# Attention output and the third normalisation in one stage, with a ring of four sets in the attention

## What is computed

```python
def _L1_attn_ref(x, w_q, w_k, w_v, w_o):
    ...
    scores = jnp.einsum('bhqd,bhkd->bhqk', q, k) / jnp.sqrt(jnp.float32(D_K))
    attn = jax.nn.softmax(scores, axis=-1)
    out = jnp.einsum('bhqk,bhkd->bhqd', attn, v)
    out = out.transpose(0, 2, 1, 3).reshape(B, S, HIDDEN)
    return jnp.einsum('bse,oe->bso', out, w_o)
...
x = _layernorm(x + _L1_attn_ref(x, ...), axis=-1)
x = _layernorm(x + _L1_ffn_ref(x, w1, w1_scale, w3, w3_scale, w2, w2_scale), axis=-1)
```

## Time and profile before

| what | us |
|---|---|
| median of 3 runs | 2102.09 |
| the profiled execution | 2091.79 |
| its span, first to last instruction | 2090.1 |
| attention, first score matmul to last quotient | 1025.8 to 1445.4 |
| attention output, first transpose to last sum | 1445.8 to 1501.6 |
| third normalisation | 1501.9 to 1571.4 |
| MLP, from its first matmul | 1571.7 to the end |

### The profile page before, as it was taken

How to read it: one execution, slowest core, us unless ns; L and a number is a source line. 1 busy time by engine, 2 the same in 40 slices (tenths; PEclk the granted TensorE clock), 3 DMA queues, 4 the chain that set the end, 5 groups by cost and what they waited for, 6 DMA issues and landing times. The chain is left out here.

```text
span 2090.1 us, 24698 instructions
## 1 busy us (share of the span) xinstructions
PE 1727.8 (83%) x7763; PEld 1052.6 (50%) x7763; DVE 1571.3 (75%) x2847; ACT 839.0 (40%) x1404; POOL 783.8 (38%) x467
## 2 busy tenths in 40 slices
PE   5888878675698994399688888888728999999998
PEld 1232323223376883288433333334616787778786
DVE  6999999998537996821288888884596667766668
ACT  5646464443114773122157777775231111111112
POOL 4898989892235996420110000000024213311200
PEclk8999989998799997599789999999858999999999
DMA  4343343320126995355533333330001000000002
GB/s 131 98 119 114 103 126 90 92 69 32 57 111 272 411 411 196 112 198 196 174 92 87 94 94 92 87 87 4 32 0 61 28 4 31 31 1 31 1 1 81
DMA packets 110653, 211.59 MB, mean 101 GB/s; under 512 B 18890, under 2 KB 35658, under 8 KB 109628
## 3 DMA queue, kind: packets, MB, share of 16 engines
q1 hardware_dynamic: 105403, 193.23, 28.4%
q0 software_dynamic: 5120, 16.78, 2.5%
HBM read 144.87 MB, written 62.65 MB: 99 GB/s over the span
## 5 line engine op out<-in xcount | busy, mean ns | idle before, releaser
L1784 DVE TENSOR_REDUCE att_top<-att_first 128x1 f32<-128x512 f32 x512 | 332.2, 686 | 101.8 <-PE att_first L1664 94.3
L551 DVE TENSOR_TENSOR_SCAN ssm_h<-ssm_da,ssm_dbx 128x512 f32<-128x512 f32 x256 | 304.6, 1207 | 6.4 <-ACT ssm_da L421 6.1
L291 POOL TENSOR_TENSOR ssm_dbx<-ssm_u,ssm_bbc 128x2048 f32<-128x2048 f32 x63 | 285.3, 4528 | 47.4 <-DVE ssm_h L551 47.0
L634 PE MATMUL ssm_y<-ssm_hc,all_ident 128*128 128x512 f32 x396 | 225.4, 657 | 77.1 <-DVE ssm_hc L502 71.0
L1746 ACT ACTIVATE att_prob<-att_second 128x1024 f32<-128x1024 f32 x256 | 248.1, 1022 | 86.1 <-PE att_second L1684 80.8
L421 ACT ACTIVATE ssm_da<-ssm_dt,ssm_minus_a 128x512 f32<-128x512 f32 x256 | 176.7, 690 | 199.3 <-DVE ssm_h L551 199.0
L1930 POOL TENSOR_TENSOR pairs_raw<-pairs_raw,pairs_scales 128x512 f32<-128x512 f32 x42 | 42.5, 1046 | 531.8 <-DMA pairs_raw<-in_w 531.8
L2060 ACT ACTIVATE ffn_silu<-ffn_pg 128x256 f32<-128x256 f32 x112 | 43.2, 385 | 415.0 <-PE ffn_pg L129 414.9
L1664 PE MATMUL att_first<-att_ks,att_qs 48*128 48x512 f32 x512 | 133.3, 510 | 63.1 <-DVE att_top L1784 48.3
L127 PE MATMUL ffn_pg<-pairs_wh,last_XH 128*128 128x512 f32 x448 | 180.2, 402 | 1.7 <-PEq L676 1.7
L128 PE MATMUL ffn_pg<-pairs_wl,last_XH 128*128 128x512 f32 x448 | 178.9, 399 | 0.0
(11 more groups left out here) (301 smaller groups left out, 3807.5 us busy)
## 6 DMA issues: line engine op xcount, KB each, us to landing
all_X<-in_w SPq DMA_DIRECT2D x33, 769.0 KB, 9.1
ssm_bbc<-brow_dram SPq DMA_DIRECT2D x64, 256.0 KB
ssm_cbs<-crow_dram SPq DMA_DIRECT2D x58, 256.0 KB, 3.5
mlps_raw<-in_w SPq DMA_DIRECT2D x16, 769.0 KB, 9.1
att_qs<-qk_dram SPq DMA_DIRECT2D x192, 64.0 KB, 2.2
att_ks<-qk_dram SPq DMA_DIRECT2D x192, 64.0 KB, 2.2
sorted_x<-ssm_zero SPq DMA_DIRECT2D x47, 256.0 KB, 3.7
exp_x<-sorted_x SPq DMA_DIRECT2D x47, 256.0 KB, 9.6
```

The costliest lines, as they stand in the source:

```text
L291: nc.gpsimd.tensor_tensor(dbx[:, n % 2], u[:, n // STATE % 2], bbc[:, n % RING, :].unsqueeze(1).to_broadcast([P, KC, NB]), ALU.mult).then_ ...
L551: nc.vector.tensor_tensor_scan(h[:, n % 2, c, :], da[:, i % 2, :], dbx[:, n % 2, c, :], 0.0, ALU.mult, ALU.add).then_inc(h_ready, 1)
L634: pe.matmul(y[:, c, :], g.ident[:], hc[:, k % 2, :], start=(m == 0), stop=(m == STATE - 1)).then_inc(y_own, 1)
L1784: nc.vector.tensor_reduce(top[w % 2][:, qt, item:item + 1], p_first[first_place(m) % FIRSTS][:], AX.X, ALU.max).then_inc(max_done, 1)
```

## The change

The two stages become one, `out_and_normalise`: per tile PE transposes, adds the residual by a matmul of g.X with the identity into the same PSUM tile (L1889 of the new kernel) and makes the 12 matmuls; DVE takes the statistics and centres straight from PSUM (a ring of four tiles), and the addition (L1889 before) and ACT's copy of the rows (L855) are gone. The MLP adds its first pair's result to g.X in place of g.Y. The buffers of the MLP's weights (`PairWeights`) now exist during the attention: the output weights and the split rows borrow room in them, and the first MLP weights are loaded by SP ahead of its iteration s = 2 and split by POOL in the attention. The attention's ring has 4 slots.

```diff
@@ -1519,7 +1519,7 @@
         PAIRS = SET // 2
         ROWS = P // 2
         SETS = BATCH * HEADS // SET
-        RING = 5
+        RING = 4
         STEPS = 4
         LEAD = 8
         TOTAL = SETS * STEPS
@@ -1617,8 +1617,10 @@
                     sp.dma_start(ks[slot][at:at + 2 * SET, :, :].bitcast(F32), select[:, k, :, :].bitcast(F32)
                                  ).then_inc(selected, 16)
             load_max(sp, 0)
-            g.wo.load(sp, a["woT"])
+            g.pair_weights.load_wo(sp)
             for s in range(SETS):
+                if s == 2:
+                    g.pair_weights.first_loads(sp)
                 if s + 1 < SETS:
                     load_max(sp, s + 1)
                 if s + RING - 1 < SETS:
@@ -1633,7 +1635,8 @@
...
-            g.wo.split(pool)
+            g.pair_weights.split_wo(pool)
+            g.pair_weights.first_split(pool)
...
-def attention_out(nc, a, g):
+def out_and_normalise(nc, a, g):
 
     with ExitStack() as ctx:
-        sb, ps, sem = scoped(nc, ctx, "wo")
-        wh, wl = g.wo.hi, g.wo.lo
-        th = sb("th", [P, 2, KC, P], F32R)
-        tl = sb("tl", [P, 2, KC, P], F32R)
+        sb, ps, sem = scoped(nc, ctx, "out")
+        f = g.pair_weights
+        wh, wl = f.wo_hi, f.wo_lo
+        th, tl = (w[:, f.WO:f.WO + 2 * DIM].rearrange("p (s c k) -> p s c k", s=2, k=P) for w in (f.wh[1], f.wl[1]))
...
+        RING = 4
         pt = [ps(f"pt{k}", [P, KC, P]) for k in range(2)]
-        po = [ps(f"po{k}", [P, DIM]) for k in range(2)]
...
+        po = [ps(f"po{k}", [P, DIM]) for k in range(RING)]
+        px = [ps(f"px{k}", [P, KC, P]) for k in range(2)]
...
         block = ctx.enter_context(nc.Block())
+
+        def each(n, *stages):
+
+            for lag, do in stages:
+                if 0 <= n - lag < TILES:
+                    do(n - lag)
 
         @block.tensor
         def _(pe):
...
-                if t:
-                    m = t - 1
-                    if m >= 2:
-                        pe.wait_ge(added, m - 1)
-                    pe.wait_ge(lo_ready, m + 1)
-                    for c in range(KC):
-                        w = slice(c * DIM, (c + 1) * DIM)
-                        mm = three(pe, po[m % 2][:], th[:, m % 2, c, :], tl[:, m % 2, c, :], wh[:, w], wl[:, w],
-                                   c == 0, c == KC - 1)
-                    mm.then_inc(product, 1)
...
+            def outputs(t):
+                pe.wait_ge(tl_ready, t + 1)
+                if t >= RING:
+
+                    pe.wait_ge(x_ready, t - RING + 1)
+                pe.matmul(po[t % RING][:], g.ident[:], g.X[:, t, :], start=True, stop=False)
+                for c in range(KC):
+                    w = slice(c * DIM, (c + 1) * DIM)
+                    mm = three(pe, po[t % RING][:], th[:, t % 2, c, :], tl[:, t % 2, c, :], wh[:, w], wl[:, w],
+                               False, c == KC - 1)
+                mm.then_inc(product, 1)
+
...
+            turn(0)
+            for n in range(TILES + 3):
+                each(n, (-1, turn), (0, outputs), (1, turn_x))
 
         @block.scalar
         def _(act):
-            for t in range(TILES):
...
+            act.wait_ge(eps_ready, 1)
+            turned_hi(0)
+            for n in range(TILES + 3):
+                each(n, (-1, turned_hi), (0, root), (1, x_hi))
 
         @block.vector
         def _(dve):
...
-                    dve.wait_ge(product, m + 1)
-                    nc.vector.tensor_tensor(g.Y[:, m, :], po[m % 2][:], g.X[:, m, :], ALU.add).then_inc(added, 1)
...
+            def variance(t):
+                dve.wait_ge(product, t + 1)
+                nc.vector.bn_stats(stats[:, t, :], po[t % RING][:]).then_inc(stats_ready, 1)
+                dve.wait_ge(stats_ready, t + 1)
+                nc.vector.bn_aggr(mv[:, t, :], stats[:, t, :]).then_inc(var_ready, 1)
+
+            def centre(t):
+                dve.wait_ge(std_ready, t + 1)
+                nc.vector.reciprocal(rstd[:, t:t + 1], std[:, t:t + 1]).then_inc(rstd_ready, 1)
+                dve.wait_ge(rstd_ready, t + 1)
+                nc.vector.tensor_scalar(g.X[:, t, :], po[t % RING][:], mv[:, t, 0:1], rstd[:, t:t + 1], ALU.subtract,
+                                        ALU.mult).then_inc(x_ready, 1)
+
...
+            turned_lo(0)
+            for n in range(TILES + 3):
+                each(n, (1, centre), (1, largest), (-1, turned_lo), (1, block_scale), (1, quantised), (2, x_lo), (0, variance))
 
 
...
+        self.wo_raw, self.wo_hi, self.wo_lo = (w[:, 0:self.WO] for w in (self.raw, self.wh[1], self.wl[1]))
+        self.wo_in, self.wo_hi_ready, self.wo_lo_ready = sem("wo_in"), sem("wo_hi_ready"), sem("wo_lo_ready")
         self.w_in, self.sc_in = sem("w_in"), sem("sc_in")
         self.scaled, self.hi_ready, self.split_ready = sem("scaled"), sem("hi_ready"), sem("split_ready")
 
+    def load_wo(self, sp):
+        sp.dma_start(self.wo_raw.rearrange("p (c e) -> p c e", c=KC),
+                     self.a["woT"].rearrange("(c p) e -> p c e", p=P)).then_inc(self.wo_in, 16)
+
...
     def first_loads(self, sp):
+
+        sp.wait_ge(self.wo_lo_ready, 1)
         sp.dma_start(self.scales[:], self.a["scales"].partition_broadcast(P)).then_inc(self.sc_in, 16)
         self.load(sp, 0)
 
@@ -2107,7 +2218,8 @@
                 if n >= TILES:
 
                     dve.wait_ge(y_added, n - TILES + 1)
-                nc.vector.tensor_tensor(g.Y[:, t, :], py[n % 2][:], g.Y[:, t, :], ALU.add).then_inc(y_added, 1)
+                base = g.X if n < TILES else g.Y
+                nc.vector.tensor_tensor(g.Y[:, t, :], py[n % 2][:], base[:, t, :], ALU.add).then_inc(y_added, 1)
 
...
         with ExitStack() as last:
-            g.wo = Ahead(nc, last, "wo_ahead")
+            sb, _, _ = scoped(nc, last, "last")
+            g.pair_weights = PairWeights(nc, last, a)
             attend(nc, a, g)
-            attention_out(nc, a, g)
-        with ExitStack() as later:
-            sb, _, _ = scoped(nc, later, "last")
             g.XH = sb("XH", [P, KC, TOK], F32R)
             g.XL = sb("XL", [P, KC, TOK], F32R)
-            g.pair_weights = PairWeights(nc, later, a)
-            normalise(nc, g, "ln3", False, quantise=True,
-                      ahead=(g.pair_weights.first_loads, g.pair_weights.first_split))
+            out_and_normalise(nc, a, g)
             quantised_mlp(nc, a, g, out)
```

More of the change, by code:

```diff
@@ L1876, in _, with root, x_hi @@
                     act.wait_ge(product, t - 1)
-                nc.scalar.activation(th[:, t % 2], pt[t % 2][:], ACT.Copy).then_inc(hi_ready, 1)
+                nc.scalar.activation(th[:, t % 2], pt[t % 2][:], ACT.Copy).then_inc(th_ready, 1)
+            def root(t):
+                act.wait_ge(var_ready, t + 1)
+                nc.scalar.activation(std[:, t:t + 1], mv[:, t, 1:2], ACT.Sqrt, bias=eps[:, 0:1]).then_inc(std_ready, 1)
+            def x_hi(t):
+                act.wait_ge(x_turned, t + 1)
+                nc.scalar.activation(g.XH[:, :, t * P:(t + 1) * P], px[t % 2][:], ACT.Copy).then_inc(xh_ready, 1)
@@ L1879, in _ @@
+            act.wait_ge(eps_ready, 1)
+            turned_hi(0)
+            for n in range(TILES + 3):
+                each(n, (-1, turned_hi), (0, root), (1, x_hi))
         @block.vector
         def _(dve):
[L1881 to L1887, removed]
-                    dve.wait_ge(product, m + 1)
-                    nc.vector.tensor_tensor(g.Y[:, m, :], po[m % 2][:], g.X[:, m, :], ALU.add).then_inc(added, 1)
+            nc.vector.memset(eps[:], EPS).then_inc(eps_ready, 1)
@@ new lines, in block_scale, with quantised @@
+            def block_scale(t):
+                dve.wait_ge(amax_ready, t + 1)
+                nc.vector.tensor_scalar(scale[:, t, :], amax[:, t, :], 1.0 / FP8_MAX, 1e-12, ALU.mult,
+                                        ALU.add).then_inc(scale_ready, 1)
+                dve.wait_ge(scale_ready, t + 1)
+                nc.vector.reciprocal(inv[:, t, :], scale[:, t, :]).then_inc(inv_ready, 1)
+            def quantised(t):
+                dve.wait_ge(inv_ready, t + 1)
+                if t >= 2:
+                    dve.wait_ge(x_turned, t - 1)
+                for c in range(KC):
+                    cols = slice(c * P, (c + 1) * P)
+                    ins = nc.vector.tensor_scalar(xq[:, t % 2, cols], g.X[:, t, cols], inv[:, t, c:c + 1],
+                                                  scale[:, t, c:c + 1], ALU.mult, ALU.mult)
+                ins.then_inc(xq_ready, 1)
@@ L1892, with x_lo @@
+            def x_lo(t):
+                dve.wait_ge(xh_ready, t + 1)
+                cols = slice(t * P, (t + 1) * P)
+                nc.vector.tensor_tensor(g.XL[:, :, cols], px[t % 2][:], g.XH[:, :, cols].bitcast(F32),
+                                        ALU.subtract).then_inc(xl_ready, 1)
+            turned_lo(0)
+            for n in range(TILES + 3):
```

(1 more changed line is left out.)

49 lines of the change are left out of this document (40 added, 9 removed).

## The result

The changed kernel takes **2197.0 us** in the median of 4 runs (2177.5 to 2198.0), the kernel before 2104.3 beside it (2102.0 to 2109.3): 1.0415 times as long, 95% interval 1.0353 to 1.0477, so 93 us slower. The forecast was 2167, slower.

What follows compares the result with a forecast made beforehand. PE and DVE in lockstep bound the attention; the stages behind it run one after the other. 56.6 + 13 - 2.0 + 23 - 25.7 = +64.9 us, against the 2102.1 median: 2167 us, range 2134 to 2196.

Steps and rivals of the forecast that it cites:

- The ring's stall: Attention: with four slots PE waits 1.95 us for each of 29 loads, +56.6 us.
- The closed loop: Attention: copy_rows, maxima, 12 issues, landing, first, turned maxima, copy_rows; lost time isn't made up inside the set.
- The long issues: Attention, SP's queue: loads that take longer to issue, hidden now, would stand in the loop, +13 us.
- the -2.0 us at the start: Attention's start: fewer DMAs ahead of the first maxima, for which PE waits 1.99 us, so -2.0 us.
- The clock: Attention: PE's clock falls to half after two stalls of three, 0.8 us a set, +23 us.
- The upper bound of 38 us: Attention: most that PE's lower clock could cost, 29 x 1.3 us, with 3 to 3.4 us at half clock.
- The joined stage: Attention's end to MLP: DVE sets the pace at 5.54 us a tile, -25.7 us.
- Zeros: Parts priced at nothing: POOL's split in the attention (up to 2 us), ACT's copy of rows, the MLP's addition.
- The signs: Expected trace: attention 70 to 105 us longer, 29 att_ks waits of 2 to 3.5 us, 98 to 103 us to MLP.
- Four slots are enough: Attention: rival with no stall, only the gain is seen, 2074 us; chance 0.08.
- No clock: Attention: rival in which the stall comes but PE's clock stays up, 2144 us; chance 0.30.
- The clock in the joined stage: Rival: lower clock holds on, in the joined stage too (15 x 2 = 30 us), 2200 us or more; chance 0.10.

Runs made afterwards that it cites:

- run 5: The changed kernel with 2 identity matmuls (4 instructions) ahead of each of the 29 waits for a set's q and k: 2134.7 us, ratio 1.0216.
- run 3: The kernel before with four ring slots and the load issued ahead of the maxima, the two stages apart: 2107.2 us, ratio 1.001.
- Run 2: The changed kernel with the load of set s+3 issued ahead of the maxima of set s+1 instead of behind them: 2076.5 us, ratio 0.9861.
- run 10: The changed kernel with the load ahead of the maxima, measured again on one chip beside another version: 2077.9 us, ratio 0.9860.

## Why the prediction was right, and where it was off

**The ring's stall: right in mechanism and in size, but not term by term.** The closed loop is there as described, 29 waits, one a set. Run 5 shows it at full clock; PE's `first` of two sets on end that nothing disturbs:

```profile
1209.25 0.50 PE L1671 MATMUL att_first<-att_ks,att_qs 48*128 48x512 f32 x2
...
1223.51 0.50 PE L1671 MATMUL att_first<-att_ks,att_qs 48*128 48x512 f32 x2
```

Such a set takes 14.26 us, and 12.31 in the kernel before: 1.95 us more, as I had it. It is made of 2.10 us from `copy_rows` to the load, 5.57 for the 12 issues, 1.73 to PE, where I had 1.74, and 4.86 to the next `copy_rows`. In the changed kernel six sets wait longer for the data to land. One of them, SP's k part and PE:

```profile
1333.98 2.75 SPq L1594 DMA_DIRECT2D att_ks<-qk_dram  x6
...
1339.87 0.79 PE L1667 MATMUL att_first<-att_ks,att_qs 48*128 48x512 f32 x2 [3.76 <-DMA att_ks<-qk_dram]
```

Here it is 3.14 us from the last issue to PE, and in the six sets 8.6 us more than 1.74 each. No term of mine had that. The long issues, which I put at 13 us, cost 8.8. And the -2.0 us at the start did not come: PE's wait for the first maxima is gone, but up to the `first` of set 3 the changed kernel takes 46.1 us, 41.9 without the stall of 4.2 us in front of it, and the kernel before 42.1. In sum the stall's own share is 56.6 + 8.8 + 8.6 = 74.0 us, where my terms have 56.6 + 13 - 2.0 = 67.6, and with the 45.1 us of the clock nearly all of the 121.0 is accounted for. The overpriced long issues hid about half of the missing term, and that is luck.

**The clock: right in kind, half its size.** The term was 23 us, and 45 were measured. The step that failed is "if 3 to 3.4 us at half clock follow each stall", with two stalls of three. From 1100 to 1400 the clock was 0.83, so 2 x 0.17 x 300 = 102 us at the lower level in about 18 sets: 5.6 us a set, where my step has 2.1. The stretch that isn't made up lost 1.6 us a set, where I had 0.8. The earlier trace rows is one fall of the clock: it could show that a short gap can be enough and how long that one lasted, and not how long the others would. It did not show either that such a gap is always enough: a gap of 1.27 us ahead of 136.36 in the same trace left the clock at 1.00. The upper bound of 38 us rested on the same 3.4 us and was no bound.

The Trainium skill, TensorE: Matmul & The Clock Gate, section HAM oscillation, asks to keep idle gaps under a few microseconds, and by it most of these gaps would cost nothing. That does not hold here. The 29 waits are 0.6 to 4.2 us, 15 of them between 2 and 3, and run 5 shows the price. Windows of the changed kernel behind a wait of 2.05 us (ahead of 1191.68) and behind one of 2.50 (ahead of 1471.03):

```profile
1193.20:1199.90 6.70, 6.70 (x26) 2.43 (x26) 3.87 (x8) 3.42 (x5) 0.00 (x0) 0.50 0.00 1
1471.00:1478.00 7.00, 6.43 (x42) 2.36 (x46) 5.55 (x11) 4.51 (x6) 0.00 (x0) 1.00 0.10 27
```

Behind the shorter wait the clock fell, behind the longer it didn't. Behind 24 of the 29 it did; the other five are the two of under 1 us and three of 2.0 to 2.5. What decides between these stays open.

**The joined stage: right, and 4.6 us better than forecast by its first tile.** The tile was priced at 5.54 us and took 5.48; DVE paces it. The centring from PSUM took 0.81 us as priced, and the last tile and the way to the MLP from its reciprocal 6.15 us, as in the sum (3.3 + 2.85). Off was the first tile: its reciprocal came 7.6 us behind the attention's end, not 11.4. The first product came at full clock, 6.3 us behind the end in place of 8.8, which was luck (below): the profile before begins its stage at the lower clock. Like with like the stage gave 26.3 us with both at full clock (runs 3 and 2) and 27.8 with both at the lower one (127.3 before, 99.5 in run 10), not 30.3. ACT loads its table ahead of the root's wait, beside PE (1.3 us). PE was mis-priced as well: the identity product is two instructions and 1.02 us, and PE's busy time 76.4 / 16 = 4.8 us a tile, not "at most 4.2". It was still under DVE's, so it cost nothing.

**Zeros.** POOL's split in the attention cost 1 to 2 us, within the 2 that I gave it, but its absence from the next stage was worth 6: I counted the move only where it went, and not where it had been, though the slow tiles of the old normalisation were in the trace. My -25.7 had it in it unnamed, since the joined tiles were priced from undisturbed rows. The MLP's -5.9 us I did not foresee: "the MLP's addition has the same shape: zero" looked at the instructions and not at the addresses.

**The base.** The terms on the profiled execution make +64.9; measured without the first line of the table is +84.8, and the difference is +21.7 (clock) and +8.7 (stall) by the split of run 5, -4.6 and -5.9. The other 8 of the 93 us must be in the first line, 19.5 us between the two profiles; the medians are nearer to each other than the profiles, because the profiled execution of before lay 10 to 18 us under its other runs. No trace of those shows why.

**The signs.** The waits on att_ks are there, 29 of them, but they and the attention's growth, 121 us, go beyond the 2 to 3.5 and the 70 to 105 that I had named. From the attention's end to the MLP are 96.0 us, 2 under the 98 to 103.

**The rivals.** Four slots are enough: out, the 12 issues are late in 29 sets of 29. No clock: out by run 5. The clock in the joined stage: out, 0.98 there. In sum the median lies 1 us over the range's upper end, carried there by the clock and the pause.

## What to carry to other kernels

A ring that is one slot shorter costs nothing as such (run 3), and 126 us if its refill is queued behind a wait for the consumer's own progress: look first at what the refill is queued behind, and move it. A stall on TensorE must be priced with the time after it at the lower clock, here about 1.6 us a set on top of 2.6; if it can't be removed, idle matmuls in it win some of it back. Price a moved piece of work at both places.

## What was not expected of the hardware

- Gaps of some 2 to 4 us, once in 16 us with TensorE dense in between, held its clock at 0.83 on average; with four 0.5 us matmuls in each gap it was 0.99. One gap of 2.05 us lowered it and one of 2.50 didn't.
- The same 12 DMAs were usable 1.7 us after the last issue in most sets, and 3.0 to 3.5 us after it in six of 29.
- The joined stage began at full clock in three of the nine profiles that have it (1.00 in its first 7 us, first reciprocal 8.6 us behind the attention's last transpose), in the other six at a lower one (0.58 to 0.83 over 8 to 10 us), and the reciprocal came at 10.3 to 11.3 us. Run 2 and its repetition, one kernel, are of different kinds. With a late first tile the changed kernel would have had some 2.5 us less gain here. The kernel before is no different: its profile begins the stage at 0.54 (1446 to 1453), that of run 3 at 1.00.
- Matmuls of one shape took 393 or 398 ns in the median by the order in which their buffers were allocated.
- A product of f32 rows with the identity, 128 x 512, is issued as two instructions, 1.02 us together (in the attention ten took 4.53 us).
- Beside POOL's arithmetic four scaled rows of DVE, with source and destination in SBUF, took 4.68 us in place of 1.12, while the statistics from PSUM kept 0.69 us. So did the block maxima, which read 512 columns from SBUF beside POOL too: SBUF as the source is not enough for the delay.
